# A graph-network kernel on one core: radial pairs in the first attention, edge sums in the second, rows fetched in the table stage, a shorter search

## What is computed

```python
x = _layernorm(x + L0(x, ...))   # two heterogeneous attention layers, then h @ ff_w + ff_b
x = _layernorm(x + L1(x, ...))   # edge sums and neighbour sums, two dense layers
x = _layernorm(x + L2(x, ...))   # messages weighted by a radial network of the edges
x = _layernorm(x + L3(x, ...))   # two graph convolutions with batch norm
```

```python
k, q, v = (typed_linear(x, ntype, W).reshape(n, H, HS) for W in (Wk, Wq, Wv))
kT = jnp.einsum('nhd,htdo->nhto', k, Watt)      # every node under each of 32 relations
vT = jnp.einsum('nhd,htdo->nhto', v, Wmsg)
kw, m = kT[src, :, etype], vT[src, :, etype]
a = jnp.einsum('ehd,ehd->eh', kw, q[dst]) * pri[:, etype].T / SQRT_D
hag = segment_sum((m * edge_softmax(a, dst, n)[:, :, None]).reshape(-1, H * HS), dst, n)
h = silu(typed_linear(hag, ntype, Wa))          # then gate, residual, layer norm
```

## Time and profile before

| what | value |
|---|---|
| time, median of 3 runs | 3235.64 us (3227.74 to 3242.81) |
| the profiled execution's own time | 3245.87 us |
| its span in the profile | 3244.2 us |
| granted TensorE clock, mean of the span | 0.818 |
| busy share of the span: PE, DVE, POOL, ACT | 77%, 62%, 62%, 44% |
| stages to qkv0, in us from the span's start | idx to 140, qkv0 140 to 224 |
| first layer | tab0 224 to 518, att0 518 to 1061, upd0 1061 to 1161 |
| second layer | qkv1 1161 to 1244, tab1 1245 to 1544, att1 1544 to 2095, upd1 2095 to 2216 |
| behind it | open 2217 to 2295, the rest 2295 to 3244 |

### The profile page before, as it was taken

The page is one execution under the profiler, slowest core; times in us unless marked ns, Lnnn a source line. Parts: engine busy times, 40 slices in busy tenths (PEclk is TensorE's granted clock), DMA queues, the critical chain, the costliest instruction groups (busy, mean ns, idle before and its releaser), DMA issues. The chain is left out here.

```text
span 3244.2 us, 52779 instructions
## 1 busy us (share of the span) xinstructions
PE 2492.4 (77%) x14692; PEld 1922.0 (59%) x14692; DVE 2008.5 (62%) x4643; ACT 1440.9 (44%) x3085; POOL 2017.4 (62%) x1928
## 2 busy tenths in 40 slices
PE   1679994777776677997677777374787999996887
PEld 1456664777775345665577777333674666664676
DVE  6764444777775475443677777344436888886444
ACT  0134443555553563443455555254443555553444
POOL 5467886777777657886777777655106777775000
PEclk9975556899898886555899899686888999997898
DMA  9869997778886657999687877565636666663653
GB/s 291 227 202 375 381 388 215 227 226 230 224 229 153 157 137 278 390 357 339 183 232 222 230 224 225 131 92 185 171 110 172 192 191 195 193 194 100 244 192 121
DMA packets 557663, 715.66 MB, mean 221 GB/s; under 512 B 126898, under 2 KB 441849, under 8 KB 531557
## 3 DMA queue, kind: packets, MB, share of 16 engines
q1 hardware_dynamic: 210932, 424.05, 38.4%
q0 software_dynamic: 107392, 156.15, 20.9%
q10 hardware_dynamic: 239104, 132.59, 14.0%
HBM read 331.57 MB, written 381.07 MB: 220 GB/s over the span
## 5 line engine op out<-in xcount | busy, mean ns | idle before, releaser
L1792 POOL DMA_INDIRECT att_rows<-table,kvrow x784 | 743.5, 948 | 274.0 <-issue 233.7
L1819 PE MATMUL att_pq<-wide,att_near 128*128 x1568 | 358.3, 314 | 274.9 <-DVE att_prod L2010 125.6
L2427 POOL DMA_INDIRECT msg_rows<-rows,msg_src x392 | 384.4, 981 | 261.6 <-DMA msg_src<-in_src_pt 142.4
L1562 POOL DMA_INDIRECT matrix<-count,place x294 | 459.5, 1563 | 89.5 <-issue 88.8
L1632 DVE COPY tab_part<-tab_bank 128x512 f32<-128x512 f32 x400 | 257.3, 686 | 322.0 <-DMA table<-tab_part 270.5
L1819 PEld LDWEIGHTS att_pq<-wide,att_near 128*128 128x128 f32 x1568 | 265.0, 212 | 307.3 <-issue 304.8
L1673 PE MATMUL tab_bank<-wk,tab_kv 32*128 32x256 f32 x1600 | 363.0, 694 | 33.1 <-DVE tab_part L1632 24.2
L1657 ACT ACTIVATE tab_part<-tab_bank 128x512 f32<-128x512 f32 x400 | 221.6, 594 | 320.5 <-DMA table<-tab_part 291.5
L1821 PE MATMUL att_pq<-wide,att_far 128*128 x1568 | 336.3, 300 | 0.0
L1673 PE MATMUL tab_bank<-wv,tab_kv 32*128 32x256 f32 x1600 | 331.4, 617 | 0.0
L1673 PEld LDWEIGHTS tab_bank<-wk,tab_kv 32*128 32x128 f32 x1600 | 203.8, 301 | 183.3 <-DVE tab_part L1632 154.8
(11 more groups left out here) (475 smaller groups left out, 5484.4 us busy)
## 6 DMA issues: line engine op xcount, KB each, us to landing
table<-tab_part SPq DMA_DIRECT2D x200, 1024.0 KB
att_sums<-att_out ACTq DMA_DIRECT2D x196, 272.0 KB
gcn_cells<-matrix SPq DMA_DIRECT2D x50, 808.0 KB
att_message<-in_ea_rows SPq DMA_DIRECT2D x98, 256.0 KB
sums<-att_out ACTq DMA_DIRECT2D x98, 256.0 KB
msg_hidden<-hidden SPq DMA_DIRECT2D x196, 128.0 KB
sums<-msg_out ACTq DMA_DIRECT2D x98, 256.0 KB
nb_cells<-matrix SPq DMA_DIRECT2D x25, 808.0 KB
```

Source lines behind the costliest of these rows:

```text
L1562: nc.gpsimd.indirect_dma_start(D.matrix, place, K.count[:, col:col + 1], None, compute_op=ALU.add).then_inc(added[b % BLOCKS], 16)
L1792: nc.gpsimd.indirect_dma_start(rows[g % RR][:, j, :], None, D.table, bass.IndirectOffsetOnAxis(ap=K.kvrow[:, t:t + 1], axis=0)).then_inc(r ...
L1819: nc.tensor.matmul(pq[g % 2][:, j * P:(j + 1) * P], near[g % RE][:, j, :], queries[:, bass.ds(window[j], 1), :].rearrange("p t d -> p (t d ...
L2427: nc.gpsimd.indirect_dma_start(rows[g % RR][:, j, :], None, D.rows, bass.IndirectOffsetOnAxis(ap=src[:, t:t + 1], axis=0)).then_inc(rows_i ...
```

## The change

- **Search.** Three small instructions take the place of six in each turn: the count as before, then (found >= 256) times a table `K.aside`, then the sum with the cell, written as an integer. `K.aside` is made once in idx by one subtraction of 128x392.
- **project** no longer fetches, turns or copies key and value. The relation weights of the first layer are loaded by SP, behind the wipes, where ACT's queue issued them before.
- **relation_table** fetches: POOL sends the 25 gathers of 128x384 first, then the scatters of the queries, then its counts. PE turns key and value of the next tile in its last quarter into bank 7, and ACT copies both in one activation after its fourth eviction. The loops over tiles are written out.
- **attention.** All edge attributes are added up in the second layer (every group), none in the first. A group leaves in one store, of 136 columns per row in the first layer and 264 in the second. The 49 radial pairs run in the first attention, one of their two layers per group, through the bank that held the edge sums; their weights are laid out on the host, and SP loads the features and stores the results. In the first attention Exp and Silu alternate on ACT.
- **update** has no radial work any more. In the second layer its gathers bring rows of 264 columns, and SP stores the edge part and the new row side by side in rows of 1024 bytes.
- **first_rows** has 25 gathers of these pair rows where there were 50.
- `COUNTS` has other sizes: qkv0 28 (was 24), tab0 144 (156), att0 22 (20), upd0 12 (8), qkv1 26 (24), tab1 122 (132), att1 22 (20), upd1 16 (8).

The diff, cut to what the text speaks of:

```diff
-COUNTS = {"qkv0": range(0, 24), "tab0": range(24, 180), "att0": range(180, 200), "upd0": range(200, 208),
-          "qkv1": range(208, 232), "tab1": range(232, 364), "att1": range(364, 384), "upd1": range(384, TILES)}
+COUNTS = {"qkv0": range(0, 28), "tab0": range(28, 172), "att0": range(172, 194), "upd0": range(194, 206),
+          "qkv1": range(206, 232), "tab1": range(232, 354), "att1": range(354, 376), "upd1": range(376, TILES)}
...
+            link(nc.vector.tensor_tensor(K.aside[:, :].rearrange("p (b n) -> p b n", n=STREAMS),
+                                         K.place[:, 0:STREAMS].unsqueeze(1).broadcast_to([P, TURNS, STREAMS]),
+                                         K.cell[:, :].rearrange("p (b n) -> p b n", n=STREAMS), ALU.subtract))
...
-    nc.vector.tensor_scalar(S.again[:, :], S.found[:, :], 256.0, None, ALU.is_ge).then_inc(S.counted, 1)
     if i >= 1:
         dve.wait_ge(S.placed, i)
-    nc.vector.tensor_tensor(S.away[:, :], K.spare[:, turn * SEEK % STREAMS:turn * SEEK % STREAMS + SEEK], K.cell[:, part], ALU.subtract).then_inc(S.counted, 1)
-    dve.wait_ge(S.counted, 5 * i + 3)
-    nc.vector.tensor_tensor(S.away[:, :], S.away[:, :], S.again[:, :], ALU.mult).then_inc(S.counted, 1)
-    dve.wait_ge(S.counted, 5 * i + 4)
-    nc.vector.tensor_tensor(S.away[:, :], S.away[:, :], K.cell[:, part], ALU.add).then_inc(S.counted, 1)
-    dve.wait_ge(S.counted, 5 * i + 5)
-    nc.vector.tensor_copy(K.place[:, part], S.away[:, :]).then_inc(S.placed, 1)
+    nc.vector.scalar_tensor_tensor(S.away[:, :], S.found[:, :], 256.0, K.aside[:, part], ALU.is_ge, ALU.mult).then_inc(S.counted, 1)
+    dve.wait_ge(S.counted, 2 * i + 2)
+    nc.vector.tensor_tensor(K.place[:, part], S.away[:, :], K.cell[:, part], ALU.add).then_inc(S.placed, 1)
...
             count_tiles(nc, K, D, pool, turns, added)
-            for u in range(RO):
-                pool.wait_ge(stored[u], 16 * len(range(u, n, RO)))
-            for t in range(NT):
-                nc.gpsimd.indirect_dma_start(rows[:, t, :], None, D.qkv,
-                                             bass.IndirectOffsetOnAxis(ap=K.slot[:, t:t + 1], axis=0)).then_inc(fetched[t // J], 16)
...
+            for t in range(NT):
+                nc.gpsimd.indirect_dma_start(rows[:, t, :], None, D.qkv,
+                                             bass.IndirectOffsetOnAxis(ap=K.slot[:, t:t + 1], axis=0)).then_inc(fetched[t], 16)
             pool.wait_ge(K.cleared, 16)
             for t in range(NT):
+                pool.wait_ge(fetched[t], 16)
...
+            def load(t):
+                act.wait_ge(flipped, t + 1)
+                nc.scalar.activation(kv[t % 2][:, :, :], bank[7][:, 0:2 * P].rearrange("p (k n) -> p k n", k=2), ACT.Copy).then_inc(node_in, 1)
...
+                    if c == 3 and t + 1 < NT:
+                        load(t + 1)
...
+            def flip_in(t):
+                pe.wait_ge(fetched[t], 16)
+                if t >= 1:
+                    pe.wait_ge(evac_high, t * 8 - 4)
+                for k in range(2):
+                    last = nc.tensor.transpose(bank[7][:, k * P:(k + 1) * P], rows[:, t, (k + 1) * P:(k + 2) * P], K.ident[:, :])
+                last.then_inc(flipped, 1)
...
+                            if k == 0 and q % 2 and quad == 3:
+                                pe.wait_ge(node_in, t + 1 + (q == Q - 1 and t + 1 < NT))
...
         def wide(h):
-            return h % LAYERS == l
...
+            return l == LAYERS - 1
...
+        def first_at(g):
+            return [v for v in range(pairs) if 2 * v + AFTER == g]
+
+        def second_at(g):
+            return [v for v in range(pairs) if 2 * v + AFTER + 1 == g]
...
+            def first_layer(v):
+                if v == 0:
+                    pe.wait_ge(net_in, 48)
+                pe.wait_ge(feat_in[v // STACK % RF], 16 * (v // STACK // RF + 1))
+                if v >= 1:
+                    pe.wait_ge(lit2, v)
+                nc.tensor.matmul(po[2][:, :], a1[:, v % STACK, :], feat[v // STACK % RF][:, :], start=True, stop=True).then_inc(hid1, 1)
+
+            def second_layer(v):
+                pe.wait_ge(lit1, v + 1)
+                nc.tensor.matmul(po[2][:, :], a2[:, :], h1[:, :], start=True, stop=True).then_inc(hid2, 1)
...
-                act.dma_start(sums[h], out[k][:, :, 0:V]).then_inc(stored[k], 16)
-                if wide(h):
-                    act.dma_start(edge_sums[h], out[k][:, :, V:WIDE]).then_inc(edge_stored[k], 16)
+                act.dma_start(sums[h], out[k][:, :, 0:OWN]).then_inc(stored[k], 16)
...
+                if store:
+                    sp.wait_ge(fetched[k], 16 * J)
+                    sp.dma_start(out[k][:, :, P:2 * P], got[k % 4][:, :, V:OWN]).then_inc(edges_out[k % 4], 16)
...
-                    nc.gpsimd.indirect_dma_start(h_rows[:, t, :], None, D.h_slots,
-                                                 bass.IndirectOffsetOnAxis(ap=K.slot[:, t:t + 1], axis=0)).then_inc(hidden_in[k], 16)
-                for t in range(tiles(k).start, tiles(k).stop):
-                    nc.gpsimd.indirect_dma_start(e_rows[:, t, :], None, D.sums,
-                                                 bass.IndirectOffsetOnAxis(ap=K.end[:, t:t + 1], axis=0)).then_inc(edges_in[k], 16)
+                    nc.gpsimd.indirect_dma_start(pair_rows[:, t, :], None, D.h_slots,
+                                                 bass.IndirectOffsetOnAxis(ap=K.slot[:, t:t + 1], axis=0)).then_inc(rows_in[k], 16)
```

307 lines of the change are left out of this document (123 added, 184 removed).

## The result

The change brings the kernel from 3238.16 us to **3221.55 us** (medians of 5 runs each on one chip; 3212.67 to 3223.74 after): a ratio of 0.9949, 95% interval 0.9932 to 0.9967. That is 16.6 us, half a per cent, where 76 had been forecast, and it lies above the range's upper end of 3212.

The account below looks back on a forecast made before the run. Stages were taken as bound one by one: tables by DMA, attentions by POOL, updates by radial pairs, projections by the fetch. Ten stage terms sum to -76 us, giving 3160 for the median (forecast 3140 to 3180), range 3125 to 3212.

Parts of the forecast that it names:

- the one on the updates: Updates: bound by the radial pairs; without them they end with POOL's counts, -22 us in upd0 and -36 in upd1.
- the 36: upd1: without the pairs it ends behind POOL's 16 counts, at 2180 against 2216, so 36 us less.
- idx -3: Index stage: the shorter search saves 3 us, bounds 0 to 5.6.
- qkv0 -17: First projection: without the fetch it ends with DVE's scaling, 17 us less, bounds -10 to -18.
- qkv1 -11: Second projection: without the fetch it ends with DVE's scaling, 11 us less, bounds -6 to -11.
- open -13: First rows: half the gathers go, so 13 us less, bounds -6 to -17.
- The tables' +12 and +13: tab0 and tab1: 25 more gathers less the dropped counts add 12 and 13 us, bounds +5 to +31 per stage.
- att0's +2: First attention: pairs hide behind POOL's gathers; two more counts at the end cost 2 us, bounds 0 to +4.
- att1's -1: Second attention: POOL still paces; two more counts, four scatters fewer, 1 us less, bounds -3 to +49.
- Rival 1: Second attention becomes bound by DMA; 10% slower would be 49 us, total 3209; chance 0.14.
- Rival 2: Table stages: transposes and ACT's wait aren't covered, 18 us more per stage, total 3196; chance 0.08.
- Rivals 4 and 5: First attention: ACT bounds it, 3176, chance 0.05; PE and ACT hand one bank over in series, 3274, chance 0.04.

Follow-up runs that it names:

- x2_warm_pe: The changed kernel with three unread 128x512 products on PE behind each block's products in both updates: 3213.51 us, ratio 0.9928.
- x7_no_lookahead: The changed kernel with each block's transposes directly ahead of its own products in both updates, on PE and ACT: 3184.49 us, ratio 0.9859.
- x13_search_only: The kernel before the change with the three-instruction search and nothing else: 3221.22 us beside 3234.77, ratio 0.9962.
- x17_search_moved_back: The kernel before with the shorter search, plus an unused tile of 10 columns in the place of the spare table: 3228.02 us beside 3226.59.
- x3_fewer_pairs: The changed kernel with 42 of the 49 radial pairs in the first attention, a constant tile replacing the last seven results: 3213.69 us, ratio 0.9928.
- x16_before_last_tile_first: The kernel before with the last edge tile's count sent first of the eight in the second update: 3239.84 us, ratio 1.002.

## Why the prediction was wrong

**The step that failed** is the one on the updates: "Without the pairs upd0 ends with POOL", and "about 10 us behind the last gather the root can start". It was read from the busy times and from the last instructions: ACT's last Silu was a radial one, so the pairs were taken for what bounds the stage. What should have been read is the chain of one block, from its scaling to its blend, and its period, 6.9 us before the change, which is longer than the 5.01 in which POOL brings a block's four tiles. The pairs filled the waits of a chain that set the end by itself: without them the block still takes about 6.85 us at a clock of 0.79 (x2_warm_pe). Taking them away left the chain, and lowered the clock under it from 0.84 to 0.52, 1 us more per block. Of the 26.2 us missed in upd0, x7_no_lookahead brings 23.2 back (81.4 beside the forecast 78). The remaining 3 are on ACT's way, not POOL's: in that run the root starts 16 us behind the last gather (1108.1 to 1124.2), not 10, and DVE's last product ends the stage.

**upd1** failed in the same step, and in a second: "some 3.5 for the last to land" was taken over from upd0, while the last tile needs about 19 (x7_no_lookahead). And the 36 were counted from one execution's 121.9, where kernels with the same update have 108 to 111, so that 12 us weren't there to be gained as a rule; the change's 109.7 is no real gain. Chain cut and last tile first give 86.7 beside the forecast 85. So the forecast of both updates was that of a kernel whose blocks keep POOL's pace and whose counts land at once, and two more edits bring it there within 3 us.

**The other terms.** idx -3 (-3.7), qkv0 -17 (-17.6), qkv1 -11 (-10.9) and open -13 (-14.8) hold, each read from what ended the stage before. The tables' +12 and +13 came out as +7.2 and +6.8, inside their bounds. The tables of before were 4.8 and 6.5 us shorter in x13_search_only, by the place of tiles as far as x17_search_moved_back tells. Beside those of x13_search_only the change's are 12.0 and 13.4 longer, and POOL's way from a table stage's start to its last count is 11.3 and 12.8 longer than in either kernel, close to the 11.8 and 13.1 worked out. That speaks for a fetch that costs 12 and for tiles that happen to lie well in the change, so that 5 to 6 us of each stage would be luck; no run shows it. att0's +2 was +8.5: the body hides the pairs, as argued, but the step left out that ACT runs six of the radial Silu behind the last gather, where nothing covers them (x3_fewer_pairs). The two more counts, which were the +2, cost nothing in either attention: behind them POOL waits for ACT, 11.40 us in att0 and 12.91 in att1 (timeline of POOL, the first scatter of att1):

```profile
2084.61 0.99 POOL L1721 DMA_INDIRECT att_sums<-att_message,first_end  x1 [12.91 <-ACT att_message L1931]
```

att1's -1 was +2.9: the stretch behind the gathers, to that scatter, took 54.6 us instead of 47.3, and the four scatters fewer gave 4.7 back. The scatter now follows the message of the edge part, some 2 us behind the other two; the other 5 come earlier in the stretch, and what makes them stays open. The rest, which the change leaves as it was, took 953.6 instead of 948.6; the other kernels built on the change have 950 to 958, and why stays open.

**The rivals.** None of the five is what happened. Rival 1: att1's gathers take 491.2 us as before (490.9), with the DMA share at 0.89 and 277 GB/s, close to the 278 worked out. Rival 2: DVE still waits for stores. Rivals 4 and 5: att0's gathers kept their pace. On the price of a table load ACT's timeline in att0 says:

```profile
1003.33 0.69 ACT L1891 ACTIVATE att_h<-att_po_edge,att_bb 128x512 f32<-128x512 f32 x1 [0.50 <-ACT att_out L1866]
1004.04 1.28 ACT L1841 ACT_TABLE_LOAD   x1
1005.33 0.31 ACT L1841 ACTIVATE att_weight<-att_less 64x128 f32<-64x128 f32 x1
```

The Silu ends at 1004.02, the load starts at 1004.04 and the exponent at 1005.33: 1.28 us and nothing else. The Trainium skill (ScalarE: Activation LUTs, section What ACT_TABLE_LOAD costs) adds a drain of about the load's size, which this row doesn't have: here the measurement decides.

**What the parts are worth.** By the table of stages the fetch's move, with the shorter turns of the search, gains 28.5 us in the projections and pays 14.0 in the tables; the pair rows gain 14.8 in open, the search 3.7 in idx. Against that stand 11.4 in the attentions, 4.2 in upd0 and 5.0 in the rest, and nothing in upd1: 12 us net, beside the measured 16.6. Most of the expected gain was to come from moving the pairs, and that only comes out with two more edits: the ratio goes from 0.9949 to 0.9859 with the blocks in plain order and to 0.9795 with the last tile first.

## What to carry to other kernels

An engine that is busy to the end of a stage need not bound it: before work is moved out, follow one period of the remaining loop through all engines, and see whether the waits that the work filled are its own or those of a chain. A look-ahead that is written into an in-order queue fits the work it was tuned beside; when that work leaves, try the plain order too. And put the one transfer that lands late first, not last, in a stage that waits for all of them, if nothing else ends the stage: in the kernel before it gained nothing (x16_before_last_tile_first).
